# A delay-attention chain: its correlation read straight from PSUM, and its VectorE steps put at other places of the queue

## The chip, the cores and the metric

The kernel runs on one core of one Trainium2 chip. The metric is the device time of one execution in microseconds. A core has the engines TensorE (PE), VectorE (DVE), ScalarE (ACT), GpSimd (POOL) and the queue processor SyncE (SP); each works through its own instructions in order, and semaphores order the engines among each other.

## The reference

Two layers over 128 sequences of 64 rows by 128 features. Layer 0 is attention and a mixture of 64 experts, layer 1 an attention by delays and a ternary product. Only layer 1's attention matters here:

```python
Qf = jnp.fft.rfft(Q, axis=2)
Kf = jnp.fft.rfft(K, axis=2)
corr = jnp.fft.irfft(Qf * jnp.conj(Kf), n=Lx, axis=2)
corr_mean = corr.mean(axis=-1)
...
top_w, top_idx = jax.lax.top_k(corr_mean, top_k)     # top_k = 4
top_w = jax.nn.softmax(top_w, axis=-1)
...
for i in range(top_k):
    gidx = (pos[None, None, :] - top_idx[:, :, i, None]) % Lx
    rolled = jnp.take_along_axis(V, gidx[..., None], axis=2)
    out = out + top_w[:, :, i, None, None] * rolled
```

For each sequence and each of 16 heads, the circular correlation of Q and K over 64 delays is averaged over the head's 8 features, the four best delays are taken, and their softmax weighs four rolled copies of V.

## The kernel before

The program has four stages one after the other: attention of layer 0, the experts, `tail` (layer 1's attention, its normalization and the largest absolute value) and `ternary`. The change lies in `tail`, at 1107 to 1291 us of the profiled span.

`tail` works on 32 pairs of tiles (N = 32; a tile is 128 rows, two sequences). It is a software pipeline written out by hand: each engine has a loop over the steps s = 0 to 45, and in step s it does stage k for pair n = s - k. `on(s, k)` says whether that pair exists. So the text of each loop is that engine's queue. For a pair: normalize (VectorE, stage 0, line 1220), transform over the rows (TensorE 1, line 1548, result `pf`), copy `xf` (ScalarE 1, line 1490), project (TensorE 2, lines 1580 to 1582, result `pq`), six copies into `qkv` (ScalarE 2, lines 1507 to 1509), products `l_pp` (GpSimd 2, line 1349), sums over a head's features (VectorE 3, line 1449); later the weighing `l_rr` (GpSimd 9, line 1325, two instructions), back transform `po` (TensorE 10, line 1560), copy `oT` (ScalarE 10), output projection `py` (TensorE 11, lines 1539 and 1540), addition to `x_res` (VectorE 11, line 1425), statistics (1433), their aggregation (1442), `rstd` (GpSimd 11, line 1358), `zn` (VectorE 12, line 1456), a transpose `pt` (TensorE 13), `xnT` (ScalarE 13, line 1517) and `amax` (VectorE 14, line 1462).

The delay chain runs once for a group of four pairs (8 groups, g = 0 to 7), as 128 partitions (8 tiles by 16 heads) by 2 sequences by 64 delays. `group(s, k)` gives g in step 4g + k, else None. Before the change:

- end of step 4g+6: TensorE correlates (line 1597) into `pc`, 128 columns of the PSUM tile `pd`; ScalarE copies it to the SBUF tile `ext` (line 1529). `ext` has 68 columns a sequence: the last four hold a sentinel of 3e38, set once, so that the eight that a search finds are these four and the four best delays.
- end of step 4g+7: VectorE searches (MAX8, line 1395), shifts by the best value (line 1400, into `e`) and marks the found entries (MATCH_REPLACE8, line 1405, into `rep`). ScalarE takes `exp` of `e` (line 1522) behind all of its other work of the step.
- step 4g+8: VectorE chooses (`rep` unequal to `ext`, line 1373), keeps (times `e`, line 1378), totals (1382), inverts (1386) and scales (1390), with the pair's work between them; TensorE then transposes `w` (line 1574) ahead of its projections of that step, ScalarE copies it to `cT` (1500), and TensorE transforms it (1588) into `pab`, which ScalarE copies to `cf` (1513). GpSimd uses `cf` from step 4g+9 on.

All of `pc`, `pw` and `pab` are parts of `pd`, one PSUM bank.

Of the kernel before, what the change touches and what calls it, by code (L numbers as in the profile page):

```python
# [28 lines left out]
ACT = mybir.ActivationFunctionType  # L29
AX = mybir.AxisListType  # L30

P = 128
S = 64
# [1191 lines left out]
def tail(nc, cst, entry, x_res, y_mean, y_rstd, xnT, amax, sem):  # L1225
# [13 lines left out]
    with ExitStack() as mem:  # L1239
        def sb(name, shape, dt=F32):  # L1240
            return mem.enter_context(nc.sbuf_tensor(name, shape, dt))
# [5 lines left out]
        qkv = sb("l_qkv", [P, SLOTS, 2, 4, D])  # L1247
        pp = sb("l_pp", [P, 2, 2, 2, D])
        sums = sb("l_sums", [P, 2, 2, G * H])
        ext = sb("l_ext", [P, 2, EXT])  # L1250
        rep = sb("l_rep", [P, 2, EXT])
        m8 = sb("l_m8", [P, 2, TOP])
        e = sb("l_e", [P, 2, S])
# [19 lines left out]
        py = psum("l_py", [P, 2, D])  # L1273
        pt = psum("l_pt", [P, 2, P])
        pd = psum("l_pd", [P, 4, P])
        pc, pw, pab = pd[:, 0, :], pd[:, 1, :], pd[:, 2:4, :]

        loaded, normed = entry.loaded, entry.normed
        transformed = sem("l_transformed")
# [4 lines left out]
        summed = sem("l_summed")  # L1284
        preset = sem("l_preset")
        correlated = sem("l_correlated")
        ext_out = sem("l_ext_out")
        top = sem("l_top")
        shifted = sem("l_shifted")
        marked = sem("l_marked")  # L1290
# [28 lines left out]
        def group(s, lag):  # L1319

            return (s - lag) // 4 if s >= lag and (s - lag) % 4 == 0 and (s - lag) // 4 < N // 4 else None
# [7 lines left out]
        with nc.Block() as block:  # L1329
# [39 lines left out]
            def _(dve):  # L1369
# [20 lines left out]
                    nc.vector.tensor_tensor(w[:], w[:], wrec[:].unsqueeze(2).to_broadcast([P, 2, S]), ALU.mult).then_inc(weights, 1)  # L1390

                def top_of(g):
                    dve.wait_ge(ext_out, g + 1)
                    for b in range(2):
                        ins = nc.vector.max(out=m8[:, b, :], in_=ext[:, b, :])
                    ins.then_inc(top, 1)
# [9 lines left out]
                                                      imm_value=-SENTINEL)  # L1406
                    ins.then_inc(marked, 1)

                nc.vector.memset(ext[:, :, S:], SENTINEL).then_inc(preset, 1)
                for s in range(STEPS):  # L1410
                    g = group(s, 8)
                    if g is not None:
                        choose(g)
                    if on(s, 0) and s >= 2:
                        n = s
                        if n == N - 2:
                            dve.wait_ge(y_rooted, 3)
                        dve.wait_ge(transformed, n - 1)
                        entry.norm_in(x_res, y_mean, y_rstd, n)
                    if g is not None:  # L1420
                        keep(g)
                    if on(s, 11):
                        n = s - 11
                        dve.wait_ge(o_projected, n + 1)
                        nc.vector.tensor_tensor(x_res[:, 2 * n:2 * n + 2, :], x_res[:, 2 * n:2 * n + 2, :], py[:], ALU.add).then_inc(added, 1)
                    if g is not None:
                        add_up(g)
                    if on(s, 11):
                        n = s - 11
                        dve.wait_ge(added, n + 1)  # L1430
# [1 line left out]
                        for j in range(2):  # L1432
                            ins = nc.vector.bn_stats(st[:, n % 2, j, :], x_res[:, 2 * n + j, :])
                        ins.then_inc(stats, 1)
                    if g is not None:
                        invert_sum(g)
                        scale(g)
                    if on(s, 11):
                        n = s - 11
                        dve.wait_ge(stats, 2 * n + 1)  # L1440
# [18 lines left out]
                    if on(s, 14):  # L1459
# [1 line left out]
                        dve.wait_ge(z_out, n + 1)  # L1461
                        nc.vector.tensor_reduce(amax[:, n:n + 1], xnT[:, 2 * n * P:2 * (n + 1) * P], AX.X, ALU.max,
                                                apply_absolute_value=True)
                    g = group(s, 7)
                    if g is not None:
                        top_of(g)
                        shift(g)
                        mark(g)
                    if s == 3:
                        dve.wait_ge(y_turned, 1)  # L1470
                        nc.vector.tensor_tensor(x_res[:, LAST, :], x_res[:, LAST, :], pd[:], ALU.add).then_inc(y_added, 1)
                    if s == 4:
                        dve.wait_ge(y_added, 1)
                        for j in range(4):
                            ins = nc.vector.bn_stats(y_st[:, j, :], x_res[:, TILES - 4 + j, :])
                        ins.then_inc(y_stats, 1)
# [6 lines left out]
            @block.scalar  # L1483
            def _(act):
                for s in range(STEPS):
                    if on(s, 1):
                        n = s - 1
                        act.wait_ge(transformed, n + 1)
                        at_least(act, projected, 2 * (n - 1))
                        nc.scalar.copy(xf[:, n % 2], pf[n % 2][:]).then_inc(f_out, 1)  # L1490
                    if on(s, 10):
                        n = s - 10
                        act.wait_ge(inverted, n + 1)
                        at_least(act, o_projected, n - 1)
                        nc.scalar.copy(oT[:, n % 2], po[:]).then_inc(o_out, 1)
                    g = group(s, 8)
                    if g is not None:
                        act.wait_ge(w_turned, g + 1)
                        at_least(act, c_transformed, g)
                        nc.scalar.copy(cT[:], pw).then_inc(w_out, 1)  # L1500
                    for j in range(2):
                        if on(s, 2):
                            n = s - 2
                            at_least(act, mixed, n - SLOTS + 1)
                            at_least(act, products, n - SLOTS + 1)
                            act.wait_ge(projected, 2 * n + j + 1)
                            nc.scalar.copy(qkv[:, n % SLOTS, j, 1:4, :], pq[j][:])
                            nc.scalar.copy(qkv[S:, n % SLOTS, j, 0, :], pq[j][0:S, 1, :])
                            nc.scalar.copy(qkv[0:S, n % SLOTS, j, 0, :], pq[j][S:, 1, :]).then_inc(q_out, 1)  # L1509
                        if g is not None and j == 0:  # L1510
                            act.wait_ge(c_transformed, g + 1)
                            at_least(act, mixed, 4 * (g - 1))
                            nc.scalar.copy(cf[:, g % 2].rearrange("p i t h -> p i (t h)"), pab).then_inc(c_out, 1)
                    if on(s, 13):
                        n = s - 13
                        act.wait_ge(z_turned, n + 1)
                        nc.scalar.activation(xnT[:, 2 * n * P:2 * (n + 1) * P], pt[:], ACT.Identity,
                                             bias=cst["ln_beta"][:], scale=cst["ln_gamma"][:]).then_inc(z_out, 1)
                    g = group(s, 7)
                    if g is not None:  # L1520
                        act.wait_ge(shifted, g + 1)
                        nc.scalar.activation(e[:], e[:], ACT.Exp).then_inc(exped, 1)
                    g = group(s, 6)
                    if g is not None:
                        act.wait_ge(correlated, g + 1)
                        at_least(act, chosen, g)
                        if g == 0:
                            act.wait_ge(preset, 1)
                        nc.scalar.copy(ext[:, :, 0:S], pc.rearrange("p (b d) -> p b d", b=2)).then_inc(ext_out, 1)

            @block.tensor
            def _(pe):
                for s in range(STEPS):
# [57 lines left out]
                    if g is not None:  # L1591
                        pe.wait_ge(summed, 4 * (g + 1))
                        at_least(pe, c_out, g)
                        if g == 0:
                            pe.wait_ge(y_added, 1)
                        for i in range(2):
                            ins = nc.tensor.matmul(pc, sums[:, g % 2, i, :], cst["idft_corr"][:, i * P:i * P + P],
                                                   start=(i == 0), stop=(i == 1))
                        ins.then_inc(correlated, 1)

# [160 lines left out]
```

## Time and profile before

| | |
|---|---|
| median of three runs (lowest, highest) | 1315.44 us (1314.62, 1316.75) |
| profiled execution: whole, span | 1318.08 us, 1316.3 us |
| TensorE busy in the span | 1248.5 us, 95% |
| VectorE | 1072.9 us, 82% |
| ScalarE | 920.2 us, 70% |
| GpSimd | 761.8 us, 58% |
| mean granted clock of TensorE | 0.984 |

Busy shares are over all four stages; only the part between 1107 and 1291 us holds code that the change touches. In the rows below, an idle time in square brackets stands before the instruction on its engine, with the instruction that ended it.

### The profile page before, as it was taken

What the parts mean: (1) busy time and instruction counts of PE and PEld (TensorE: products, weight loads), DVE (VectorE), ACT (ScalarE), POOL (GpSimd) and SP (SyncE); (2) the same over time, 40 slices, a digit from 0 to 9 for tenths busy, and PEclk for the clock granted to TensorE, in tenths of its full rate; (3) what the DMA queues carried; (4) which work ended last, traced back from release to release, by engine and by line L of the source; (5) the groups of instructions that cost most, each with busy time, mean ns of one, the idle gap of its engine ahead of it and who ended that gap; (6) DMA issues with size and microseconds to landing.
All of it is one profiled execution on the core that took longest, in us unless ns stands there. A gap on an engine that the chain in (4) does not pass through costs nothing. (4 is left out here: it accounts for less than half of the span.)

```text
span 1316.3 us, 29967 instructions
## 1 busy us (share of the span) xinstructions
PE 1248.5 (95%) x9114; PEld 1004.1 (76%) x9114; DVE 1072.9 (82%) x2050; ACT 920.2 (70%) x1563; POOL 761.8 (58%) x817
## 2 busy tenths in 40 slices
PE   7999999996999999999999999999999999798976
PEld 4777777774788887788878887788888887687865
DVE  4878888885987988978977987978987976578887
ACT  3778888883776776777777776777777776766740
POOL 3765666562565655655665665755665533466770
PEclk9999999997999999999999999999999999999998
DMA  4501010101987686877687676777687683100004
GB/s 119 114 27 32 28 32 28 32 16 32 213 189 171 177 180 149 191 180 168 170 181 178 161 180 152 187 180 175 165 189 177 164 202 81 33 26 25 17 2 128
DMA packets 126150, 159.57 MB, mean 121 GB/s; under 512 B 20840, under 2 KB 59504, under 8 KB 126064
## 3 DMA queue, kind: packets, MB, share of 16 engines
q1 hardware_dynamic: 124974, 158.16, 49.8%
q8 instruction: 34, 0.56, 0.2%
q10 hardware_dynamic: 1090, 0.43, 0.1%
q14 instruction: 52, 0.43, 0.1%
HBM read 152.25 MB, written 6.29 MB: 120 GB/s over the span
## 5 line engine op out<-in xcount | busy, mean ns | idle before, releaser
L1036 DVE TENSOR_TENSOR e_m<-e_pu,raw 128x1024 f32<-128x1024 f32 x256 | 310.0, 1212 | 95.2 <-ACT e_pu L1099 67.6
L1099 ACT ACTIVATE e_pu<-e_pu 128x1024 f32<-128x1024 f32 x256 | 258.6, 1010 | 161.3 <-PE e_pu L1135 159.6
L1109 ACT CAST e_mh<-e_m 128x1024 fp32r<-128x1024 f32 x256 | 268.1, 1047 | 47.0 <-DVE e_m L1036 45.5
L955 POOL TENSOR_TENSOR e_ml<-e_m,e_mh 128x1024 fp32r<-128x1024 f32 x80 | 193.0, 2415 | 125.2 <-ACT e_mh L1109 125.0
L1041 DVE TENSOR_TENSOR e_ml<-e_m,e_mh 128x1024 fp32r<-128x1024 f32 x176 | 238.8, 1357 | 21.6 <-ACT e_mh L1109 20.8
L1133 PE MATMUL e_pu<-r_xh,wuh 128*128 128x512 f32 x528 | 215.4, 408 | 2.6 <-PEq L208 1.9
L1144 PE MATMUL e_py<-e_mh,wdh 128*128 128x512 f32 x528 | 208.7, 395 | 3.0 <-ACT held L1086 3.0
L1134 PE MATMUL e_pu<-r_xh,wul 128*128 128x512 f32 x528 | 209.7, 397 | 0.0
L1135 PE MATMUL e_pu<-r_xl,wuh 128*128 128x512 f32 x528 | 209.6, 397 | 0.0
L1145 PE MATMUL e_py<-e_mh,wdl 128*128 128x512 f32 x528 | 209.4, 397 | 0.0
L1148 PE MATMUL e_py<-e_ml,wdh 128*128 128x512 f32 x528 | 168.4, 398 | 0.9 <-DVE e_ml L1041 0.4
L1144 PEld LDWEIGHTS e_py<-e_mh,wdh 128*128 128x128 f32 x528 | 99.4, 188 | 27.5 <-issue 4.2
L1148 PEld LDWEIGHTS e_py<-e_ml,wdh 128*128 128x128 f32 x528 | 98.3, 188 | 28.4 <-POOL e_ml L955 4.1
L1133 PEld LDWEIGHTS e_pu<-r_xh,wuh 128*128 128x128 f32 x528 | 100.1, 190 | 25.4 <-issue 2.5
L1135 PEld LDWEIGHTS e_pu<-r_xl,wuh 128*128 128x128 f32 x528 | 100.0, 189 | 24.0
L1145 PEld LDWEIGHTS e_py<-e_mh,wdl 128*128 128x128 f32 x528 | 99.3, 188 | 24.1
L1134 PEld LDWEIGHTS e_pu<-r_xh,wul 128*128 128x128 f32 x528 | 100.2, 190 | 20.9
L267 DVE TENSOR_REDUCE mx<-ps 128x16 f32<-128x1024 f32 x64 | 78.4, 1225 | 43.8 <-PE ps L530 43.8
L377 POOL TENSOR_TENSOR kx<-qkT,hmask 128x512 f32<-128x512 f32 x64 | 66.5, 1039 | 80.9 <-ACT qkT L479 79.0
L569 PEld LDWEIGHTS pob<-vx,pT 128*64 128x64 f32 x2048 | 65.1, 138 | 26.8 <-issue 20.5
L272 DVE TENSOR_TENSOR prob<-ps,mx 128x1024 f32<-128x1024 f32 x64 | 77.7, 1214 | 0.2 <-PE ppT L543 0.2
L1349 POOL TENSOR_TENSOR l_pp<-l_qkv 128x512 f32<-128x512 f32 x32 | 41.2, 1287 | 62.4 <-ACT l_qkv L1509 62.4
(229 smaller groups left out, 2397.4 us busy)
## 6 DMA issues: line engine op xcount, KB each, us to landing
raw<-gates_scratch SPq DMA_DIRECT2D x512, 256.0 KB, 4.3
x_res<-in_x_dram SPq DMA_DIRECT2D x64, 64.0 KB, 1.8
xcT<-in_ctxT_dram SPq DMA_DIRECT2D x64, 64.0 KB, 2.0
held<-in_ctx_dram SPq DMA_DIRECT2D x32, 128.0 KB, 2.1
out_dram<-t_res SPq DMA_DIRECT2D x16, 256.0 KB, 2.3
raw<-in_L_ffn_W_up_dram SPq DMA_DIRECT2D x4, 512.0 KB, 4.3
raw<-in_L_ffn_W_down_dram SPq DMA_DIRECT2D x4, 512.0 KB, 5.6
gates_scratch<-raw SPq DMA_DIRECT2D x16, 128.0 KB, 2.3
```

The lines of the kernel that those rows point to most:

```text
L267: nc.vector.tensor_reduce(by_group(mx[:, r % 2, :]), ps, AX.X, ALU.max).then_inc(maxed, 1)
L955: nc.gpsimd.tensor_tensor(flat(ml[k][:]), flat(m[k][:]), flat(mh[k][:]).bitcast(F32), ALU.subtract).then_inc(m_low[1], 1)
L1036: nc.vector.tensor_tensor(flat(m[r % 3][:]), flat(pu[r % 3][:]), flat(gt[i % SPREAD]), ALU.mult).then_inc(gated, 1)
L1041: nc.vector.tensor_tensor(flat(ml[k][:]), flat(m[k][:]), flat(mh[k][:]).bitcast(F32), ALU.subtract).then_inc(m_low[0], 1)
L1099: nc.scalar.activation(flat(pu[k][:]), flat(pu[k][:]), ACT.Silu).then_inc(silued, 1)
L1109: nc.scalar.copy(flat(mh[k][:]), flat(m[k][:])).then_inc(m_high, 1)
L1133: nc.tensor.matmul(pu[k][:, j, :], cst["wuh"][:, w], xh[:, b, :], start=True, stop=False)
L1134: nc.tensor.matmul(pu[k][:, j, :], cst["wul"][:, w], xh[:, b, :], start=False, stop=False)
L1135: ins = nc.tensor.matmul(pu[k][:, j, :], cst["wuh"][:, w], xl[:, b, :], start=False, stop=True)
L1144: nc.tensor.matmul(py[:], cst["wdh"][:, w], mh[k][:, j, :], start=(i == 0 and j == 0), stop=False)
L1145: nc.tensor.matmul(py[:], cst["wdl"][:, w], mh[k][:, j, :], start=False, stop=False)
L1148: ins = nc.tensor.matmul(py[:], cst["wdh"][:, w], ml[k][:, j, :], start=False, stop=(i == FULL))
```

## The change

The tile `ext` in SBUF goes. The name now means 136 columns of `pd` in PSUM, with the sentinels in it; TensorE correlates into them, and VectorE's search, shift, mark and choice read them there. The copy by ScalarE and its semaphore go. `pw` and `pab` share the first half of `pd`. TensorE's correlation of group g waits for the choice of the group before.

VectorE does search, shift and mark at the start of step 4g+7 instead of its end, and the choice in the same step, behind the statistics, instead of at the start of 4g+8. In step 4g+8 keep comes first, the total before the addition of `py`, the inverse before the statistics, the scaling behind them. ScalarE takes `exp` behind the copy of `oT`, ahead of the six copies, instead of at the step's end. The sentinels are set in step 4.

```diff
-        ext = sb("l_ext", [P, 2, EXT])
...
-        pc, pw, pab = pd[:, 0, :], pd[:, 1, :], pd[:, 2:4, :]
+        pab, pw = pd[:, 0:2, :], pd[:, 0, :]
+        ext = pd[:].rearrange("p j c -> p (j c)")[:, 2 * P:2 * P + 2 * EXT].rearrange("p (b d) -> p b d", b=2)
...
                 def top_of(g):
-                    dve.wait_ge(ext_out, g + 1)
+                    dve.wait_ge(correlated, g + 1)
...
-                nc.vector.memset(ext[:, :, S:], SENTINEL).then_inc(preset, 1)
                 for s in range(STEPS):
-                    g = group(s, 8)
-                    if g is not None:
-                        choose(g)
+                    marking, weighing = group(s, 7), group(s, 8)
+                    if marking is not None:
+                        top_of(marking)
+                        shift(marking)
+                        mark(marking)
+                    if weighing is not None:
+                        keep(weighing)
                     if on(s, 0) and s >= 2:
...
-                    if g is not None:
-                        keep(g)
+                    if weighing is not None:
+                        add_up(weighing)
                     if on(s, 11):
...
-                    if g is not None:
-                        add_up(g)
+                    if weighing is not None:
+                        invert_sum(weighing)
                     if on(s, 11):
...
-                    if g is not None:
-                        invert_sum(g)
-                        scale(g)
+                    if weighing is not None:
+                        scale(weighing)
+                    if marking is not None:
+                        choose(marking)
                     if on(s, 11):
...
-                    g = group(s, 7)
-                    if g is not None:
-                        top_of(g)
-                        shift(g)
-                        mark(g)
...
                     if s == 4:
                         dve.wait_ge(y_added, 1)
+                        nc.vector.memset(ext[:, :, S:], SENTINEL).then_inc(preset, 1)
...
                         nc.scalar.copy(oT[:, n % 2], po[:]).then_inc(o_out, 1)
+                    g = group(s, 7)
+                    if g is not None:
+                        act.wait_ge(shifted, g + 1)
+                        nc.scalar.activation(e[:], e[:], ACT.Exp).then_inc(exped, 1)
                     g = group(s, 8)
...
-                    g = group(s, 7)
-                    if g is not None:
-                        act.wait_ge(shifted, g + 1)
-                        nc.scalar.activation(e[:], e[:], ACT.Exp).then_inc(exped, 1)
-                    g = group(s, 6)
-                    if g is not None:
-                        act.wait_ge(correlated, g + 1)
-                        at_least(act, chosen, g)
-                        if g == 0:
-                            act.wait_ge(preset, 1)
-                        nc.scalar.copy(ext[:, :, 0:S], pc.rearrange("p (b d) -> p b d", b=2)).then_inc(ext_out, 1)
...
                         at_least(pe, c_out, g)
+                        at_least(pe, chosen, g)
                         if g == 0:
-                            pe.wait_ge(y_added, 1)
+                            pe.wait_ge(preset, 1)
                         for i in range(2):
-                            ins = nc.tensor.matmul(pc, sums[:, g % 2, i, :], cst["idft_corr"][:, i * P:i * P + P],
+                            ins = nc.tensor.matmul(ext[:, :, 0:S], sums[:, g % 2, i, :], cst["idft_corr"][:, i * P:i * P + P],
```

## Rows read from the trace of the kernel before

**Rows 1.** Windows by stretch: bounds, length, busy us of PE, PEld, DVE, ACT, POOL, clock, DMA.

```profile
1123.00:1271.00 148.00, 125.69 (x940) 113.80 (x940) 113.66 (x376) 98.11 (x271) 93.74 (x137) 0.95 0.07 21
...
1172.00:1174.00 2.00, 2.00 (x9) 1.64 (x9) 1.54 (x6) 0.67 (x2) 0.00 (x0) 0.50 0.00 0
```

**Rows 2.** Waits, 1123 to 1271 us: total us, times, longest.

```profile
PE l_pd L1574 <- DVE l_w L1390: 19.8, 8, 3.4
```

**Rows 3.** Timeline of PE, group 4: start, us, instruction, [idle before].

```profile
1203.61 0.61 PE L1597 MATMUL l_pd<-idft_corr,l_sums 128*128 128x128 f32 x4
...
1210.49 0.38 PE L1568 MATMUL l_pt<-ident,l_zn 128*128 128x128 f32 x2
1213.49 0.33 PE L1574 MATMUL l_pd<-ident,l_w 128*128 128x128 f32 x1 [2.61 <-DVE l_w L1390]
...
1215.64 0.61 PE L1539 MATMUL l_py<-w1T,l_oT 128*128 128x128 f32 x4
```

**Rows 4.** Timeline of PE, group 2.

```profile
1171.52 0.47 PE L1574 MATMUL l_pd<-ident,l_w 128*128 128x128 f32 x1 [2.62 <-DVE l_w L1390]
...
1175.18 0.61 PE L1539 MATMUL l_py<-w1T,l_oT 128*128 128x128 f32 x4
```

**Rows 5.** Timeline of DVE, group 4, steps 4g+7 and 4g+8.

```profile
1204.95 0.59 DVE L1220 TENSOR_SCALAR held<-x_res,y_mean,y_rstd 128x128 f32<-128x128 f32 x2
1205.46 0.41 DVE L1425 TENSOR_TENSOR x_res<-x_res,l_py 128x256 f32<-128x256 f32 x1
...
1207.69 1.24 DVE L1456 TENSOR_SCALAR l_zn<-x_res,l_mv,l_rstd 128x128 f32<-128x128 f32 x2 [0.30 <-POOL l_rstd L1358]
...
1209.18 0.35 DVE L1395 MAX8 l_m<-l_ext 128x8 f32<-128x68 f32 x2
...
1210.29 0.94 DVE L1373 TENSOR_TENSOR l_w<-l_rep,l_ext 128x128 f32<-128x128 f32 x1
1211.15 0.59 DVE L1220 TENSOR_SCALAR held<-x_res,y_mean,y_rstd 128x128 f32<-128x128 f32 x2
...
1212.95 0.48 DVE L1390 TENSOR_TENSOR l_w<-l_w,l_wrec 128x128 f32<-128x128 f32 x1
```

**Rows 6.** Timeline of POOL, the same stretch.

```profile
1205.26 1.41 POOL L1349 TENSOR_TENSOR l_pp<-l_qkv 128x512 f32<-128x512 f32 x1 [0.65 <-ACT l_qkv L1509]
...
1207.63 1.22 POOL L1325 TENSOR_TENSOR l_rr<-l_qkv,l_cf 128x256 f32<-128x256 f32 x2
1209.80 1.27 POOL L1349 TENSOR_TENSOR l_pp<-l_qkv 128x512 f32<-128x512 f32 x1 [0.96 <-ACT l_qkv L1509]
...
1212.07 1.21 POOL L1325 TENSOR_TENSOR l_rr<-l_qkv,l_cf 128x256 f32<-128x256 f32 x2
```

**Rows 7.** Timeline of DVE in groups 0, 1, 6 and 7.

```profile
1129.26 0.29 DVE L1378 TENSOR_TENSOR l_w<-l_w,l_e 128x128 f32<-128x128 f32 x1 [1.84 <-ACT l_e L1522]
...
1146.71 1.18 DVE L1378 TENSOR_TENSOR l_w<-l_w,l_e 128x128 f32<-128x128 f32 x1 [0.72 <-ACT l_e L1522]
...
1148.90 0.69 DVE L1390 TENSOR_TENSOR l_w<-l_w,l_wrec 128x128 f32<-128x128 f32 x1
...
1250.72 0.97 DVE L1373 TENSOR_TENSOR l_w<-l_rep,l_ext 128x128 f32<-128x128 f32 x1
...
1267.72 0.76 DVE L1400 TENSOR_TENSOR l_e<-l_ext,l_m 128x128 f32<-128x128 f32 x1
```

**Rows 8.** Timeline of POOL, group 1.

```profile
1148.82 1.26 POOL L1325 TENSOR_TENSOR l_rr<-l_qkv,l_cf 128x256 f32<-128x256 f32 x2
```

**Rows 9.** Timeline of ACT, group 0.

```profile
1127.55 1.28 ACT L1522 ACT_TABLE_LOAD   x1
```

**Rows 10.** Timeline of PE, group 6.

```profile
1253.40 0.33 PE L1574 MATMUL l_pd<-ident,l_w 128*128 128x128 f32 x1 [2.05 <-DVE l_w L1390]
```

**Rows 11.** Timeline of ACT, group 4, steps 4g+7 and 4g+8.

```profile
1207.66 0.48 ACT L1507 COPY l_qkv<-l_pq 128x384 f32<-128x384 f32 x1 [0.69 <-PE l_pq L1582]
...
1210.22 0.30 ACT L1522 ACTIVATE l_e<-l_e 128x128 f32<-128x128 f32 x1
```

More of the change, by code:

```diff
@@ L1286, in tail @@
         correlated = sem("l_correlated")
-        ext_out = sem("l_ext_out")
         top = sem("l_top")
```

## Prediction

> **What bounds the kernel now.** I read the windows by stretch first. The delay attention of layer 1 with the steps around it fills 1107 to 1291 us of the span; its middle, 1123 to 1271 us, has TensorE busy for 126 of 148 us, VectorE for 114 and ScalarE for 98 [rows 1]. No engine is full, so something waits in turn. The chain that ended last, in the page, covers only the last stage, so I went to the waits of this stretch. TensorE waits for one thing of weight: 8 times for the scaled weights `l_w` of line 1390, 19.8 us in total [rows 2]. There is one such wait for each of the 8 groups of four steps. In the timeline of the group at 1213 us TensorE is done with its work of step 4g+8 at 1210.87, gets the transpose of `w` at 1213.49 and begins the next step at 1215.64 [rows 3]. Outside this wait it runs without a gap, so what is taken from the wait comes off the end time, if TensorE does not meet the next late thing. In the group at 1171 us the same stretch from transpose to next step takes 3.66 instead of 2.15 us [rows 4]: after its wait TensorE ran at 1.2 GHz there (granted clock 0.50 in the window 1172 to 1174 [rows 1]), 1.5 us more. Of the eight groups, three (at 1130, 1150 and 1171 us) show it.
>
> Who makes the weights late? VectorE from the step before on: its timeline of group 4 (g counted from 0) has step 4g+7 starting at 1204.95 and the scaling starting at 1212.95, with one idle gap of 0.30 us [rows 5]. So VectorE is the path from 1205 to 1213.4, and what counts is what lies in its queue before the scaling, and how long each takes. Here the durations are not constant: the two normalizations of line 1456 take 1.24 us at 1207.69, the choosing of line 1373 takes 0.94 at 1210.29, the scaling 0.48. They end where GpSimd instructions end: `l_rr` 1207.63 to 1208.85, `l_pp` 1209.80 to 1211.07, `l_rr` from 1212.07 in two halves of 0.61 [rows 6]. Instructions with an operand in PSUM are not held: the addition of `py` (line 1425) at 1205.46 takes 0.41 although `l_pp` runs from 1205.26 [rows 5, 6]. This is the key to the change: **VectorE is held by GpSimd, by instruction**, and GpSimd is timed by ScalarE's copies and so by TensorE.
>
> The Trainium skill ("SBUF — State Buffer", section "SBUF: two separate sides") has the same: a VectorE instruction with two SBUF inputs, or in a two-port mode, and a GpSimd instruction exclude one another for the whole instruction. It would let the choice from PSUM run free, as I take it from the rows.
>
> **The change part by part.**
> Moved, not removed: VectorE's work between the start of step 4g+7 and the scaling is the same set of instructions in both kernels. Before: normal work, search, shift, mark, choose, normalize, keep, add, total, statistics, inverse, scale. After: search, shift, mark, normalize, add, statistics, choose, aggregate, sums, `zn`, `amax`, then keep, normalize, total, add, inverse, statistics, scale. A shorter chain behind the correlation therefore brings nothing by itself in the groups where VectorE is full. What changes is which instructions meet GpSimd. I work group 4 through, with GpSimd's times as before, since they hang on TensorE.
> - Search, shift, mark: 1.11 us from 1209.18 to 1210.29, where the last instruction was waited for [rows 5]; without that, about 1.0. They now start at 1204.95. The correlation begins on TensorE at 1203.61 and takes 0.61 [rows 3], so it is there at 1204.22, 0.7 us before. Normalizing then starts at 1205.94 instead of 1204.95.
> - It now meets `l_pp`, which would run 1205.26 to 1206.53 (1.27, as at 1209.80; before it was held to 1.41 itself) [rows 6]. Held to 1206.6, second half 0.26 after: the addition starts at 1206.85, 1.4 later than before.
> - From the addition to `zn` it was 2.23 us with the 0.30 of waiting for `rstd` in it [rows 5]. The wait goes, since `rstd` is long there; the choice comes in with 0.2 (0.29 long, no longer held, one operand in PSUM) and covers as much of the wait for the statistics. So some 1.85: `zn` at 1208.7. It meets only the last of `l_rr` (to 1208.85), then runs its second half in 0.3; `amax` is over at about 1209.5. Before this was 1209.18.
> - Keep starts at 1209.5, 0.3 before `l_pp` (1209.80), and goes free in 0.2. The normalizing pair has its second half held until `l_pp` ends at 1211.07. From there total, add, inverse and statistics take 1.1: before, normalizing, keep and these took 1.80 from 1211.15 to 1212.95 [rows 5], of which the normalizing has 0.51 and keep 0.20. Scaling is issued at 1212.17, 0.1 after the first half of `l_rr` began; it is held to that half's end, 1212.68, and is over at 1212.85 instead of 1213.43. Gain 0.6 us, by one half of `l_rr`. That VectorE does slip in between the halves is shown in group 1: scaling issued at 1148.90, 0.69 long, over at 1149.59, with `l_rr` (two in 1.26) from 1148.82 [rows 7, 8].
>
> So a steady group (2 to 5) gives 0.6, **four of them 2.4 us**. This is a step function: keep 0.3 us later and the scaling misses that half, gain 0; scaling 0.1 us earlier and it comes before `l_rr`, gain 1.2.
> - Group 1 (weights at 1149.6): VectorE has free time. Keep waits for `exp` and is then held by `l_pp`, 1.18 us [rows 7]. After, `exp` follows 3 us earlier, keep goes before `l_pp`, and scaling can end soon after `l_pp` does, which is at 1147.9 by the end of the keep that it held, so at 1148.1: **1.4 us**.
> - Group 0: keep waits 1.84 us for `exp` [rows 7], which stands behind the six copies of `q` on ScalarE and behind a table load of 1.28 [rows 9]. After, that load and `exp` stand in front of these copies; weights are some 2 us earlier, but the copies and with them `xf` are 1.6 later and give 0.8 of it back: **1.2 us**.
> - Group 6 (wait of TensorE 2.05 [rows 10]): there is no normalizing in step 32, so keep, total, add, inverse and statistics are done when `l_pp` ends, at 1251.7 by the choice of 0.97 us from 1250.72 that it held [rows 7], and scaling with them at 1251.8 instead of 1253.40: **1.6 us**. Group 7: shift, held to 0.76 before [rows 7], reads PSUM, and the correlation is 0.7 us before VectorE's step: about **1.2 us**.
> - Clock: three of the seven first groups pay 1.5 us [rows 4]. The wait of 2.62 us at 1171 brought it, those of 2.61 at 1213 and 2.05 at 1253 did not [rows 3, 4, 10], so the wait alone does not tell. With waits of 0.5 to 2 us I take one of the three away, **1.5 us**; ends 4.5 less and 1.5 more.
> - ScalarE: the copy of `ext` goes, off the path. `exp` (0.30 [rows 11]) now stands before the copies of `q` in step 4g+7; there ScalarE has 0.69 us of waiting for TensorE [rows 11], and the shift is over at about 1205.6, 2.1 before those copies begin. Nothing, while that cover holds; without it 0.3 a group. Behind it are queued those six copies, then `l_pp`, then VectorE's sums.
> - TensorE's added wait for `chosen` of the group before is fulfilled three steps earlier. The sentinels' memset, one instruction, goes into step 4. No DMA moves. Nothing for these.
> - Reading the search's input from PSUM: no row shows MAX8 or MATCH_REPLACE from there. The nearest row is line 1425, 256 columns, one operand in PSUM, 0.41, beside a tensor_tensor of 128 columns from SBUF that nothing holds, 0.29 [rows 5, 7]: 0.12 for 128 more columns, that is no surcharge. I take 0; ends minus 0.05 and plus 0.2 an instruction (the search again as long), six instructions a group.
>
> The Trainium skill ("VectorE: DVE Perf Modes", section "The TRN2 errata") speaks against that: it gives VectorE 58 fixed cycles from SBUF and 120 from PSUM. As an estimate from that page that is 65 ns each, 0.39 us a group; line 1425 does not show it.
>
> Sum on the profiled execution: span 1316.3, less 1.2 + 1.4 + 2.4 + 1.6 + 1.2 = 7.8, less 1.5 of clock, gives 1307.0. That execution took 1318.1 with what lies around its span, the median of the runs is 1315.4; the difference is the same off either: 1315.4 - 9.3 = **1306.1**.
>
> **The rivals.**
> - A, the steady groups give nothing. Keep slips behind `l_pp` (0.3 us of room, six instructions of which each need cost only 0.05 more from PSUM), everything in front of `l_pp`'s end is lost as before, and the scaling at 1212.75 misses the half that ends at 1212.68. Left are 5.4 us and no clock: 1310.0. For it: two narrow margins. Chance 0.23. By the surcharge that the Trainium skill (same page and section) gives, keep would be at 1209.9, and this is what would come.
> - B, more than that: scaling comes before `l_rr` in the steady groups (1.2 each, 2.4 more), and the low clock is gone in all three (3.0 more): 1300.7. For it: 0.1 us is missing only, and shorter waits. Chance 0.17.
> - C, no change: the gains of the outer groups meet TensorE's own work or more low clock (up to 4 groups more at 1.5 us). Some 1315. Chance 0.10.
> - D, slower: `exp` in front of the copies holds them. The place is ScalarE's queue in step 4g+7, it decides from the point where the shift is over later than 1207.3 (0.30 before the copies at 1207.66), 1.7 us later than I reckon. Each group then pays at least 0.31 on the path to `l_pp`, on whose end the weights hang, and group 0 the table load: 8 x 0.31 + 1.28 = 3.8 with nothing gained: 1319.2. Against it: those 1.7 us. Chance 0.05.
>
> **How the numbers follow.** My case has the remaining 0.45. The range must reach A and B: 1300.5 to 1313.0 leaves out C's middle and D and a little beyond B. 0.2% is 2.6 us, about what a measurement of this kernel can tell: faster takes in my case, A, B and a little of C, 0.84; within it most of C and a rest of A, 0.11; slower 0.05.
>
> **What would show it.** In the changed profile: TensorE's waits at the transpose some 10 to 12 us in total instead of 19.8; choose at 0.29 us in all groups; in the steady groups keep (line 1378's counterpart) starting just before `l_pp`, and scaling ending with the first half of `l_rr`; no wait of keep for `exp` in groups 0 and 1; MAX8 from PSUM at 0.21 us; the rows of the granted clock at 0.5 in two groups at most. Wrong is the prediction if keep shows 1 us in the steady groups (A), if MAX8 takes markedly more, or if ScalarE waits for the shift before `exp`.

## The result, and the profile after

The changed kernel takes 1308.37 us (1306.82 to 1308.83), the kernel before, beside it on the same chip, 1316.1 us: ratio 0.994, 95% interval 0.9923 to 0.9958. Run again with the experiments it took 1306.36 us (1305.31 to 1308.62), ratio 0.9938 [0.9924, 0.9951]. Both ratios make it some 8 us faster (0.006 of 1316). Forecast were 1306.1 us and 9.3 us less.

The profiled execution took 1308.58 us, its span is 1306.8. First the busy times over the span, then the waits from 1123 to 1265 us (total us, times, longest), which answer to [rows 2] (line 1566 is before's 1574):

```profile
PE 1245.4 (95%) x9114; PEld 999.9 (77%) x9114; DVE 1070.6 (82%) x2050; ACT 918.6 (70%) x1555; POOL 761.2 (58%) x817
```

```profile
PE l_pd L1566 <- DVE l_w L1389: 11.8, 8, 2.0
```

TensorE's wait for the weights fell from 19.8 to 11.8 us: 8.0, where the terms of the groups added up to 7.8. By group (the transposes in the timeline of PE; start, us, instruction, [idle before]; groups 0, 1, 2, 4, 6 and 7):

```profile
1127.40 0.33 PE L1566 MATMUL l_pd<-ident,l_w 128*128 128x128 f32 x1 [1.50 <-DVE l_w L1389]
...
1143.59 0.33 PE L1566 MATMUL l_pd<-ident,l_w 128*128 128x128 f32 x1 [0.62 <-DVE l_w L1389]
...
1163.19 0.33 PE L1566 MATMUL l_pd<-ident,l_w 128*128 128x128 f32 x1 [1.99 <-DVE l_w L1389]
...
1204.12 0.33 PE L1566 MATMUL l_pd<-ident,l_w 128*128 128x128 f32 x1 [1.99 <-DVE l_w L1389]
...
1243.38 0.33 PE L1566 MATMUL l_pd<-ident,l_w 128*128 128x128 f32 x1 [0.41 <-DVE l_w L1389]
...
1259.66 0.33 PE L1566 MATMUL l_pd<-ident,l_w 128*128 128x128 f32 x1 [1.31 <-DVE l_w L1389]
```

| group | 0 | 1 | 2 to 5, each | 6 | 7 |
|---|---|---|---|---|---|
| wait before, us | 3.37 | 2.33 | 2.62 | 2.05 | 1.56 |
| wait after | 1.50 | 0.62 | 1.99 | 0.41 | 1.31 |
| gone | 1.87 | 1.71 | 0.63 | 1.64 | 0.25 |
| forecast | 1.2 | 1.4 | 0.6 | 1.6 | 1.2 |

The steady groups came out as worked through. VectorE in group 4, from the choice to the scaling, and GpSimd beside it, which answer to [rows 5] and [rows 6]:

```profile
1198.90 0.27 DVE L1372 TENSOR_TENSOR l_w<-l_rep,l_pd 128x128 f32<-128x128 f32 x1
...
1200.65 0.28 DVE L1377 TENSOR_TENSOR l_w<-l_w,l_e 128x128 f32<-128x128 f32 x1
1200.85 1.56 DVE L1220 TENSOR_SCALAR held<-x_res,y_mean,y_rstd 128x128 f32<-128x128 f32 x2
...
1203.38 0.69 DVE L1389 TENSOR_TENSOR l_w<-l_w,l_wrec 128x128 f32<-128x128 f32 x1
```

```profile
1201.06 1.27 POOL L1348 TENSOR_TENSOR l_pp<-l_qkv 128x512 f32<-128x512 f32 x1 [1.09 <-ACT l_qkv L1512]
...
1203.29 1.26 POOL L1324 TENSOR_TENSOR l_rr<-l_qkv,l_cf 128x256 f32<-128x256 f32 x2
```

Keep starts 0.41 us before `l_pp` and goes free in 0.28; the normalizing pair takes the hold in its place (1.56); the scaling is issued 0.09 us after `l_rr` begins and is over at 1204.07, soon after the first half of `l_rr` is (1203.92), long before the second (1204.55).

**The clock.** Windows of 2 us show a granted clock of 0.50, or up to 0.6 where a stretch straddles two windows, in three stretches of `tail` after (behind the weights of groups 3, 5 and 7), before in four: behind groups 0, 1 and 2 and at 1263 to 1268. The stretch at the very end of `tail`, where the engines wait in turn, is in every trace and is left out here. The first and the last of after (columns as in [rows 1]):

```profile
1184.00:1186.00 2.00, 2.00 (x10) 1.90 (x9) 0.80 (x3) 1.37 (x4) 0.00 (x0) 0.50 0.00 0
...
1262.00:1264.00 2.00, 1.97 (x10) 1.56 (x9) 1.62 (x8) 0.78 (x2) 1.71 (x5) 0.50 0.00 0
```

From its first transform to the transpose that ends it, `tail` takes 172.86 us instead of 181.56: 8.7 less. The 8.0 us of waits and one low stretch fewer can't simply be added to that. Before's stretch at 1263 us stands ahead of the wait of group 7 and shortens it (shown under group 7 below), so it cost 0.3 us and hides 0.75 us of waiting. Set against traces with the full clock at the same place, the schedule accounts for some 8.6 of the 8.7 us (7.76 of waits gone in groups 0 to 6, 0.9 in group 7). The low clock accounts for 0.1: the four stretches of before cost 4.8 us (1.4, 1.6, 1.5 and 0.3), the three of after 4.7 (1.8, 1.6, 1.3), by the distances between transposes. The remaining 0.8 of the span's 9.5 lies outside `tail`, where both kernels do the same.

### The profile page after: what moved, and what is told of

It reads as the page before. It is cut to its first block and busy times, and to the rows that moved or that the text cites. A ratio compares the mean times of both kernels' runs of the same rounds, so it can differ in the third digit from the quotient of the medians.

```text
span 1306.8 us, 29951 instructions
## 1 busy us (share of the span) xinstructions
PE 1245.4 (95%) x9114; PEld 999.9 (77%) x9114; DVE 1070.6 (82%) x2050; ACT 918.6 (70%) x1555; POOL 761.2 (58%) x817
## 5 line engine op out<-in xcount | busy, mean ns | idle before, releaser
L1099 ACT ACTIVATE e_pu<-e_pu 128x1024 f32<-128x1024 f32 x256 | 258.6, 1010 | 161.1 <-PE e_pu L1135 158.9
L569 PE MATMUL pob<-vx,pT 128*64 128x18 f32 x2048 | 71.3, 212 | 1.7 <-ACT vx L488 0.5
```

What stands on the lines that cost most here:

```text
L569: ins = nc.tensor.matmul(po[q, 2 * j:2 * j + 2, :], pT[:, r % 2, j, q], vx[:, r % 4, j, b], start=True, stop=True)
L1099: nc.scalar.activation(flat(pu[k][:]), flat(pu[k][:]), ACT.Silu).then_inc(silued, 1)
```

## The experiments

The runs were made in three batches (e1 to e4 and e5 to e8 on one chip, e9 to e12 on another), each beside the kernel before; across the batches only the ratios compare. Theory: VectorE is held by GpSimd instruction by instruction; the weights come when keep gets ahead of `l_pp`, and the scaling ends with a half of `l_rr`. The gain needs both halves of the change, PSUM and order. Rivals: a longer or shorter queue costs in proportion; `exp` is what matters; reading from PSUM has a price; the low clock decides.

| kernel | median, us | ratio to before [95%] | wait, steady group | all 8 waits | `tail` |
|---|---|---|---|---|---|
| e1 changed, again | 1306.36 | 0.9938 [0.9924, 0.9951] | 1.99 | 11.8 | 171.7 |
| e2 PSUM only | 1317.23 | 1.0012 [1.0, 1.0025] | 2.12 | 18.4 | 183.7 |
| e3 order only | 1312.39 | 0.9978 [0.9967, 0.9989] | 1.84 | 14.0 | 176.2 |
| e4 `exp` late | 1315.24 | 0.9997 [0.9985, 1.0009] | 2.61 | 20.0 | 180.0 |
| e5 pad 0.19 us | 1306.75 | 0.9927 [0.9909, 0.9946] | 1.99 | 12.1 | 173.0 |
| e6 pad 0.57 us | 1313.35 | 0.9973 [0.996, 0.9986] | 2.61 | 18.5 | 177.7 |
| e7 scale early | 1299.4 | 0.9872 [0.9855, 0.989] | 1.06 | 7.5 | 163.9 |
| e8 scale first | 1295.85 | 0.985 [0.9832, 0.9868] | 0.40 | 4.5 | 161.1 |
| e9 before, filled | 1314.16 | 0.9979 [0.9965, 0.9993] | 0.85 left | 8.1 | 178.3 |
| e10 e2, filled | 1310.2 | 0.9959 [0.9942, 0.9977] | 0.34 left | 6.0 | 174.7 |
| e11 changed, filled | 1304.7 | 0.991 [0.9894, 0.9926] | 0.20 left | 4.7 | 168.1 |
| e12 e2 again | 1318.67 | 1.0011 [0.9995, 1.0026] | 2.12 | 18.5 | 179.7 |

`tail` is from the trace of one execution each, low clock included.

**e1: the changed kernel again.** Waits as in the first profile to 0.01 us, low clock again behind groups 3 and 5, none behind 7. So the schedule has a part in where the stretches fall (e5 has them behind 3, 5 and 7 too), and chance another.

> The changed kernel once more, nothing edited. What is asked: how far the low-clock stretches of TensorE move from one execution to the next. If they fall by chance of phase, the weight waits repeat to 0.05 us (1.50, 0.62, four of 1.99, 0.41, 1.31) while the number of groups with 1.2 GHz after the wait is another than in the first profile (groups 3 and 5), and the time varies by about 1.5 us per such group. If they belong to the schedule, the same two groups show them again. Time 1308.4, give or take 1.

**e2: PSUM without the new order.** The tile `ext` and its copy go, every step stays where it was.

```diff
-        ext = sb("l_ext", [P, 2, EXT])
+        ext = pd[:].rearrange("p j c -> p (j c)")[:, 2 * P:2 * P + 2 * EXT].rearrange("p (b d) -> p b d", b=2)
...
-                        nc.scalar.copy(ext[:, :, 0:S], pc.rearrange("p (b d) -> p b d", b=2)).then_inc(ext_out, 1)
```

> Search, shift, mark and choice read PSUM, the copy by ScalarE is gone, but all instructions stay at their places of before (search at the end of step 4g+7, choice at the head of 4g+8, exp at the end of ScalarE's step). Theory (VectorE is held by GpSimd per instruction): the choice takes 0.28 instead of 0.94, the normalizing pair behind it is held in its place, keep starts 0.3 earlier and the scaling just reaches the first half of l_rr, so that the steady groups' waits go from 2.61 to about 2.0; groups 0 and 1 keep their wait for exp, 3.4 and 2.3 us. About 2.5 us less than before: 1313.6. Rival (only the order counts): as before, 1316. Rival (only PSUM counts): as the changed kernel, 1308.4.

```profile
1207.20 0.29 DVE L1372 TENSOR_TENSOR l_w<-l_rep,l_pd 128x128 f32<-128x128 f32 x1
1207.41 0.79 DVE L1220 TENSOR_SCALAR held<-x_res,y_mean,y_rstd 128x128 f32<-128x128 f32 x2
...
1209.41 0.30 DVE L1389 TENSOR_TENSOR l_w<-l_w,l_wrec 128x128 f32<-128x128 f32 x1
```

VectorE's timeline of group 4: the choice, 0.94 us before [rows 5], is no longer held (0.29), the next instruction, the normalizing out of SBUF, is instead (0.79). The steady waits fall to 2.12 as expected, the interval from group to group where the clock is full from 20.22 to 19.72 us. The time did not follow: 1317.2 us, not 1313.6. By the time alone the rival "only the order counts" (1316) would have won. The trace has low clock behind six of the eight groups, two of its windows being

```profile
1170.00:1172.00 2.00, 2.00 (x9) 1.83 (x8) 0.69 (x3) 1.31 (x4) 0.00 (x0) 0.50 0.01 4
...
1210.00:1212.00 2.00, 2.00 (x9) 1.63 (x9) 1.79 (x6) 0.41 (x2) 0.20 (x1) 0.50 0.00 0
```

That the low clock ate the gain was a suspicion until e9, e10 and e12.

**e3: the new order with `ext` in SBUF**, filled by ScalarE's copy as before; all of the diff's moves of VectorE's steps and of `exp` stay.

> The order of the changed kernel (search, shift, mark at the head of step 4g+7, choice behind the statistics, keep at the head of 4g+8, early exp), but ext stays in SBUF and ScalarE copies it at the end of step 4g+6 as before. Theory: VectorE now waits at the head of step 4g+7 for that copy, about 1.0 us in a steady group, the shift and the choice are held by l_pp and l_rr again, keep comes behind l_pp, and the steady groups give nothing or lose 0.5; groups 0 and 1 keep 1 to 1.5 us each for the early exp. 1313 to 1315. Rival (the order is what pays): 1308.4, with waits of 2.0 in the steady groups.

The waits for the weights are shorter than in the changed kernel in the steady groups, but TensorE waits elsewhere (waits from 1150 to 1240 us):

```profile
DVE l_m L1395 <- ACT l_ext L1529: 4.7, 5, 1.0
...
PE l_pt L1568 <- DVE l_zn L1460: 2.2, 4, 0.6
```

The search stands at the head of VectorE's step and waits there up to 1.0 us for the copy out of PSUM; everything behind it comes later, `zn` among it, and TensorE loses at its transpose (0.56 each time) what it gained. The interval between steady groups stays 20.22 us. What the order alone gives, 1.9 us at group 0 among it, lies in the outer groups. So in the steady groups the order alone gives nothing, PSUM alone 0.5 us of the 0.63, and both together the rest; the outer groups need the order. That both halves are needed everywhere, as the theory had it, is too strong. The sum shows how little each gives alone. As an estimate, take `tail` and subtract its low stretches (1.4 in e9, 1.5 in e3): before's schedule is at 176.9 us (e9), PSUM alone at 174.7 (e10), order alone at 174.7 (e3), both at 168.1 (e11). Each half alone gives 2.2 us, both together 8.8.

**e4: `exp` back behind the six copies of `q`**, the rest as changed.

```diff
-                    g = group(s, 7)
-                    if g is not None:
-                        act.wait_ge(shifted, g + 1)
-                        nc.scalar.activation(e[:], e[:], ACT.Exp).then_inc(exped, 1)
                     g = group(s, 8)
```

> The changed kernel with exp back at the end of ScalarE's step 4g+7. Theory: keep, which now stands first in step 4g+8, must wait for exp (its end about 1.1 us after keep could start), is then held by l_pp to that one's end, the normalizing pair comes whole behind it, and the scaling is issued about 0.6 later and misses the first half of l_rr: steady waits 2.6 instead of 1.99, groups 0 and 1 lose 1 to 2 us each. About 5 us more than the changed kernel: 1313. Rival (exp's place is indifferent, since the scaling hangs on the end of l_pp in either case): 1308.4.

```profile
1209.34 0.60 DVE L1377 TENSOR_TENSOR l_w<-l_w,l_e 128x128 f32<-128x128 f32 x1 [1.14 <-ACT l_e L1521]
...
1211.41 0.74 DVE L1389 TENSOR_TENSOR l_w<-l_w,l_wrec 128x128 f32<-128x128 f32 x1
```

```profile
1210.79 1.21 POOL L1324 TENSOR_TENSOR l_rr<-l_qkv,l_cf 128x256 f32<-128x256 f32 x2
```

Keep waits 1.14 us for `exp`, is held by `l_pp`, and the scaling, issued 0.01 us after the first half of `l_rr` is over, ends with the second: 2.61 again. Without `exp`'s move the whole gain is gone (ratio 0.9997; 1313 us were expected, 1315.2 came).

**e5 and e6: a useless reduction ahead of keep**, 128 columns (0.19 us to the next start) or 512 (0.57).

```diff
+                        nc.vector.tensor_reduce(spare[:], x_res[:, 0:1, :].rearrange("p t d -> p (t d)"), AX.X, ALU.add)
```

(`0:4` in e6.) They lay out rival A's point: keep had 0.41 us of room.

> The changed kernel with one useless reduction of 128 columns (about 0.2 us of VectorE, operand in no GpSimd's way) ahead of keep in step 4g+8. Theory: keep (at 1200.65 in group 4) still starts before l_pp (1201.06), the half of the normalizing pair that is held ends with l_pp as before, so 8 x 0.2 us of added VectorE work cost nothing in groups 1 to 6: steady waits 1.99. Groups 0 and 7, where nothing is held, pay 0.2 each. Rival (VectorE's work is simply the path): steady waits 2.19, 1.6 us more than the changed kernel.

> The same with a reduction of 512 columns, about 0.57 us. Theory: keep now comes 0.15 behind the start of l_pp, is held to its end, the normalizing pair follows whole, and the scaling is issued at about 1203.97, behind the first half of l_rr: steady waits 2.6, that is 0.6 more for 0.57 of work, in one jump (with the short one it was nothing). Groups 0, 1, 7: 0.6 more each, or less where exp was waited for. About 3.5 us more than the changed kernel: 1310 to 1311. Rival (work is the path): also 2.55, so only both pads together tell. Rival (scaling still meets the first half, which it misses by 0.06 only): 1.99 as before.

```profile
1202.80 0.27 DVE L1416 TENSOR_REDUCE l_spare<-x_res 128x1 f32<-128x128 f32 x1
...
1203.19 1.63 DVE L1220 TENSOR_SCALAR held<-x_res,y_mean,y_rstd 128x128 f32<-128x128 f32 x2
```

```profile
1207.25 0.33 PE L1568 MATMUL l_pd<-ident,l_w 128*128 128x128 f32 x1 [2.61 <-DVE l_w L1390]
```

With 0.19 us more (first fence) the wait is 1.99 in every steady group, as without; with 0.57 (second fence, the transpose of group 4) it is 2.61, 0.62 more: one half of `l_rr`. So the cost is a step, and not always of that size: with the same 0.57 us the waits of groups 1 and 6 went from 0.62 and 0.41 to 2.43 and 2.03, three times what was added. Group 1 was expected at 0.6 or less; e6 took 1313.4 us instead of 1310 to 1311.

**e7 and e8: the scaling earlier.** e7 puts inverse and scaling behind the total, ahead of the addition of `py` and the statistics; e8 puts total, inverse and scaling right behind keep, ahead of the normalizing.

```diff
                     if weighing is not None:
                         keep(weighing)
+                        add_up(weighing)
+                        invert_sum(weighing)
+                        scale(weighing)
```

(e8; the three go from their later places.)

> The changed kernel with total, inverse and scaling together behind the normalizing of step 4g+8, ahead of the addition of py and the statistics. Theory: scaling is issued about 0.55 earlier, at 1202.86 instead of 1203.38 in group 4, before l_rr begins at 1203.29, so it is not held: weights at 1203.15 instead of 1204.05, steady waits 1.1 instead of 1.99, four times 0.9. Group 1 and 6 as now (held by l_pp), group 7 0.6 less. About 4.3 us less than the changed kernel: 1303 to 1304. Rival (the addition and statistics, now later, make TensorE wait for py's buffer or GpSimd for the statistics): no gain, and such a wait in the trace.

> As the one before, and the normalizing pair of step 4g+8 also behind the scaling. Theory: scaling is issued at 1201.5, is held by l_pp to 1202.35, weights at 1202.45: steady waits about 0.4. VectorE then has 0.5 us more behind the weights and takes it from its idle time in step 4g+9 (0.89 and 0.81), so nearly all reaches the end: 1.3 to 1.6 us a steady group, 5 to 6 in all: 1301 to 1303. Rival (VectorE is full: what it does later in 4g+8 makes keep come behind l_pp in the next group): 0.6 to 1 of it lost again, 1304 to 1306.

The scaling of a steady group, in e7 and then in e8, and the transpose in e8:

```profile
1200.06 0.29 DVE L1389 TENSOR_TENSOR l_w<-l_w,l_wrec 128x128 f32<-128x128 f32 x1
```

```profile
1195.28 0.98 DVE L1389 TENSOR_TENSOR l_w<-l_w,l_wrec 128x128 f32<-128x128 f32 x1
...
1196.32 0.33 PE L1564 MATMUL l_pd<-ident,l_w 128*128 128x128 f32 x1 [0.40 <-DVE l_w L1389]
```

In e7 it runs before `l_rr` (1200.50), free: the wait falls by 0.93. In e8 `l_pp` holds it (0.98), which is still the earlier place: 0.40 us of waiting are left. Neither trace has a low stretch before the last 2 us of `tail`; from 1150 to 1250 us the granted clock is 1.00. Both came out faster than expected (1303 to 1304 and 1301 to 1303), since the expectations counted waits alone; the mean granted clock of their executions is 0.988 and 0.989, the changed kernel's in e1 0.984. Both beat both kernels, e8 by 0.0088 of the time, some 11 us, against the changed one.

**e9 to e11: the wait filled.** Eight useless matmuls (0.22 us each) ahead of TensorE's wait, issued once the buffer that they write is free, keep it busy while the weights come when they did: in groups 0 to 6 of the kernel before (e9) and of e2 (e10), in groups 2 to 5 of the changed one (e11).

```diff
+                        for i in range(8):
+                            nc.tensor.matmul(pq[0][:, 0, :], cst["ident"][:], cst["dft"][:, 0:P], start=True, stop=True)
```

> The kernel before with eight useless matmuls of 128 columns (into pq[0], which the next projection overwrites) ahead of TensorE's wait for the weights in groups 0 to 6. Nothing that is computed changes. Theory (the low clock of 1.5 us a group follows the idle wait): the matmuls take some 1.8 us of the 2.0 to 3.4 us of waiting, the weights arrive when they did, so nothing moves but the low stretches; those after the waits of 2.6 us (left: 0.8) go, three in the profile before, so some 4.5 us less than before, 1311. In the windows no granted clock of 0.5 between 1150 and 1260 us. Rival (the low clock has nothing to do with this idle wait, or is not what the time hangs on): the stretches stay, or go and the next wait for the weights grows by as much: 1315.5.

> The same eight useless matmuls in the kernel with only the search's input moved to PSUM (e2), groups 0 to 6. e2 had waits of 2.12 instead of 2.61 us in the four steady groups, and yet 1317.2 us, with six stretches of low clock where before had three. Theory (the gain of 0.5 us in four groups is real, and more low clock ate it): with the clock out of the way this is 2 us less than e9, and about 6 x 1.5 = 9 us less than e2: 1308 to 1309.5. Rival (reading from PSUM costs elsewhere what it gives at the choice): the same as e9, 1311 or more.

> The same eight useless matmuls in the changed kernel, in the four steady groups only (waits of 1.99 us, two of them followed by a low stretch). Theory: waits of 0.2 us are left behind the added matmuls, the two low stretches go, 3 us less than the changed kernel: 1304 to 1305. Rival (the clock is of no account): as the changed kernel, 1307 to 1308; and should the matmuls last longer than the wait, 0.1 to 0.2 a group more.

Windows of e9 from 1150 to 1250 us, and its transpose of group 4:

```profile
1150.00:1250.00 100.00, 96.30 (x782) 89.45 (x781) 85.49 (x275) 70.55 (x197) 68.02 (x100) 1.00 0.08 23
```

```profile
1208.43 0.33 PE L1578 MATMUL l_pd<-ident,l_w 128*128 128x128 f32 x1 [0.87 <-DVE l_w L1390]
```

None of the 18 filled waits of the three traces is followed by the low clock, and the kernels with useless work are faster than the same without. e11 gains 0.9938 - 0.991, that is 3.7 us, for two filled waits with a low stretch, 3.4 us together, in each profile of the changed kernel; 3 were expected. The two ran in different batches and their intervals just touch; the bare medians differ by 1.7 us. e10 gains 1.0012 - 0.9959, 7 us, where 9 were expected; its schedule is 2.2 us shorter than e9's (`tail` 174.7 against 178.3 less the one low stretch of 1.4 that e9 has in group 7), as the steady groups of e2 had promised. By the ratios it is 2.6 us, with intervals that just overlap. e9 gained only 2.8 us of 4.5 (1.3 by the medians). In its profile the three stretches behind groups 0, 1 and 2 are gone, but group 7, which is not filled, has a new one of 1.4 us; `tail` is 3.3 us shorter.

**e12: e2 once more.**

> The kernel of e2, unchanged, once more. If the place of the low stretches is set by the schedule, its profile has them in the same six groups, 0, 1, 2, 4, 6 and 7; if chance has a part, in others, at the same waits (3.37, 2.33, 2.12 four times, 2.03). The time should be that of e2, 1317.2, within 0.2%.

```profile
1168.00:1170.00 2.00, 2.00 (x17) 1.73 (x16) 1.36 (x6) 1.40 (x5) 0.00 (x0) 1.00 0.02 4
1170.00:1172.00 2.00, 2.00 (x20) 2.00 (x19) 1.16 (x5) 1.92 (x5) 1.02 (x1) 1.00 0.00 0
```

The same waits, and low clock behind groups 0, 4 and 6 only: the windows shown, at 1.00 here, were at 0.71 and 0.50 in e2. So the same schedule gets six low stretches in one execution and three in another; `tail` differs by 4.0 us. The medians agree (1317.2, 1318.7): e2's outcome is not one bad execution.

## Why the prediction came out right, step by step

- **VectorE is held by GpSimd, by instruction:** right, and enough to place keep against `l_pp` to 0.1 us (0.3 forecast, 0.41 measured) and the scaling against `l_rr` to 0.01 (0.1 and 0.09). The rule of the Trainium skill ("SBUF — State Buffer", "SBUF: two separate sides") agrees; e5 and e6 show the step that follows from it.
- **Steady groups 0.6 each:** right (0.63). Rival A was one reduction away, as e6 shows, and e4 is in its state; rival B is what e7 does.
- **No surcharge for PSUM:** right. MAX8 takes 0.35 us for two from either, MATCH_REPLACE8 0.22 instead of 0.21, the choice 0.27 instead of 0.29. The Trainium skill ("VectorE: DVE Perf Modes", "The TRN2 errata") gives 120 cycles against 58; the 65 ns more for each that the forecast estimated from that are not there.
- **`exp` ahead of the copies costs nothing:** right, rival D did not come. But it was put down as an edit at no cost, and without it nothing of the gain is left (e4).
- **Group 0, 1.2:** too small, 1.87. The 0.8 given back by a late `xf` did not come. TensorE starts the projection at 1127.57, right behind its transpose: 

```profile
1125.83 0.29 DVE L1377 TENSOR_TENSOR l_w<-l_w,l_e 128x128 f32<-128x128 f32 x1 [0.80 <-ACT l_e L1498]
```

```profile
1127.57 0.40 PE L1572 MATMUL l_pq<-w1T,l_xf 128*128 128x128 f32 x2
```

  That projection takes the `xf` of the step before, and the copies that the table load delays have until a step later. VectorE still waits 0.80 us for `exp` behind the table load (1.28).
- **Group 1, 1.4; group 6, 1.6:** 1.71 and 1.64.
- **Group 7, 1.2:** too large, though not by as much as the 0.25 of the table says. In the profile of before TensorE runs at the low clock from 1263 us on, and so comes later to its wait. The same schedule without that stretch is in e9, whose group 7 is not filled. Before, then e9, from the correlation to the transpose:

```profile
1263.17 0.99 PE L1597 MATMUL l_pd<-idft_corr,l_sums 128*128 128x128 f32 x4 [0.98 <-DVE l_sums L1449]
...
1270.89 0.33 PE L1574 MATMUL l_pd<-ident,l_w 128*128 128x128 f32 x1 [1.56 <-DVE l_w L1390]
```

```profile
1258.25 0.71 PE L1601 MATMUL l_pd<-idft_corr,l_sums 128*128 128x128 f32 x4 [0.98 <-DVE l_sums L1449]
...
1261.32 0.71 PE L1539 MATMUL l_py<-w1T,l_oT 128*128 128x128 f32 x4 [0.24 <-ACT l_oT L1495]
...
1265.64 0.33 PE L1578 MATMUL l_pd<-ident,l_w 128*128 128x128 f32 x1 [2.31 <-DVE l_w L1390]
```

  At the full clock the wait is 2.31 us and the way 7.39, in the changed kernel 1.31 and 6.51 (1253.15 to 1259.66): 0.9 us gained. The rest of the 1.2 is lost so: the search is not there at the correlation's end (1253.86), since `zn` of the step before is held to 1254.6; and with the search, 1.0 us, ahead of the addition of `py`, TensorE waits for that addition where it had waited 0.24 us for `oT`:

```profile
1256.44 0.68 PE L1531 MATMUL l_py<-w1T,l_oT 128*128 128x128 f32 x4 [0.47 <-DVE x_res L1427]
```

  The forecast had counted the instructions behind the correlation and not who waits for what they are put ahead of.
- **Clock, 1.5:** not borne out. The forecast saw three low stretches and not the fourth, at 1263 us, and took 1.5 us off for one of three. One profile has indeed one stretch fewer, but by the cost of each the two profiles differ by 0.1 us. The executions say no more: the kernel before has a mean granted clock of 0.9838 beside e1 to e4, the changed kernel 0.9838 in e1 and 0.9848 in its first four. Single executions of one kernel spread by 0.002 about that mean, and 0.001 of it is worth 1.3 us of time, so a gain of 0 to 1.5 us in the mean is open. What is taken off a median should be the change of the mean, not a count in one profile. That the profiled execution of before lay 2.6 us above the median is not shown to come from the clock either: its own, 0.984, is the mean.
- **Where luck helped:** the schedule gave some 8.6 us of forecast 7.8, most of the difference in groups 0 and 1, and the clock close to nothing of 1.5. The two errors have opposite signs, and so the 9.3 us came close to the 9.5 by which the profiled spans differ and to the 8 of the ratios.

e9 was forecast by the same count, 4.5 us. There the mean did move as forecast, from 0.9838 to 0.9872, worth up to 4.5 us, and the time fell by 2.8 only. One part may be the unfilled group 7; the rest stays open.

The mean granted clock of e2 and e12 is 0.9812 in both. 0.0026 of 1313 us are at most 3.4 us lost to the low clock beyond what before loses; the 2 us that its schedule gives are eaten by that. Filled (e10) it has 0.9867. So shorter waits (2.1 instead of 2.6 us) went with more of the low clock here; **why** stays open.

## What to carry to other kernels

Where two engines exclude one another by instruction, work out for each instruction of the chain which one of the other engine it would meet, and how much room there is to the next: e6 and e7 are one useless instruction and two places apart and differ by 14 us, 11.0 of them in the eight waits. Put the instructions that someone waits for ahead of the long ones that nobody waits for (e8), even where they are held in their turn. Take the low clock, where it comes and goes, as a mean over executions and never as the count of one profile, and look for a low stretch ahead of a wait before the wait is compared: at half the clock the engine comes later to it and the wait looks short.

## What the runs showed of the hardware

- An idle wait of TensorE is followed by a stretch of some 3 us at 1.2 GHz (granted clock 0.50) not always but with a chance. Over all traces here: behind waits for the weights of 3.37 us and more in 4 of 4, behind 1.8 to 2.7 us in 20 of 53, behind 1.3 to 1.6 us in 2 of 14, behind shorter or filled ones never. Each of these costs 1.3 to 1.8 us. That the wait is the cause is shown by e9 to e11. The length of the wait is not all that counts: in the four steady groups the changed kernel has the stretches behind groups 3 and 5 in both of its traces, while e6, with waits of 2.61 us, has none there. One stretch of before, at 1263 us, follows shorter waits of another kind (the longest 0.98 us, for `l_sums`); no other trace has one there, and its cause is open.
- Useless matmuls in that wait pay for themselves: by the ratios 3.7 us of 1308 in e11 (1.7 by the medians), 7 us in e10.
- Between two successive GpSimd instructions a waiting VectorE instruction gets in: the scaling ends with the first half of `l_rr`, while the second follows without a gap (1.26 us for both).
- Moving one operand to PSUM frees that VectorE instruction, not the queue: in e2 the choice takes 0.29 instead of 0.94 us, and the normalizing behind it is held instead (0.79).
